# All loops of a three-layer kernel written out, and its clearing transfers issued by SyncE

## The reference, cut to what matters

```python
x = x + xattn(layernorm(x), ctx_512, Wq, w_kc_q, w_kc_kv, W_qr, W_kr, Wo)   # 16 heads, 257 context rows per batch item
x = x + attn(layernorm(x), wq, wk, wv, wo (codes and scales), biases)       # self attention, 32 tokens per batch item
x = x + ffn(layernorm(x), router_weight, gate_up_proj, down_proj)           # 64 experts, top 8, capacity 128

# ffn, cut:
probs = softmax(x @ router_weight.T)
topw, topi = top_k(probs, 8); topw = topw / sum(topw)
pos = place of each (token, expert) pair in its expert's list, in token order
xe = zeros((64, 128, 256)).at[expert, pos].set(x, mode='drop')
ye = (silu(xe @ gate) * (xe @ up)) @ down
y[token] = sum over the 8 pairs of topw * ye[expert, pos]
```

## Time and profile before

| | |
|---|---|
| time, median of 3 runs | 846.65 us (844.25 to 850.82) |
| span of the profiled execution | 876.3 us |
| instructions | 17897 |
| PE, DVE, ACT, POOL busy | 76%, 48%, 35%, 33% |
| bytes moved | 92.66 MB, mean 106 GB/s |
| fold and weights, pass 0 | 0 to 151 us |
| pass 1 | 157.9 to 218.6 us |
| passes 2 to 6 (the loop) | 218.7 to 537.4 us |
| pass 7 | 537.4 to 592.1 us |
| experts and output | about 666 to 876.3 us |

### The profile page before, as it was taken

How to read it: one execution, slowest core, us unless ns; L and a number is a source line. 1 busy time by engine, 2 the same in 40 slices (tenths; PEclk the granted TensorE clock), 3 DMA queues, 4 the chain that set the end, 5 groups by cost and what they waited for, 6 DMA issues and landing times.

```text
span 876.3 us, 17897 instructions
## 1 busy us (share of the span) xinstructions
PE 664.1 (76%) x6210; PEld 536.8 (61%) x6210; DVE 420.8 (48%) x1090; ACT 305.1 (35%) x811; POOL 291.6 (33%) x279
## 2 busy tenths in 40 slices
PE   7856777889999997997997997998714765556550
PEld 5745557777867875875875875867513654445440
DVE  1414663454765774774774764756441222222232
ACT  1122553235453362362362363350302333333210
POOL 4003584212114224124124122021224455555562
PEclk8855657799999998998998998999966999999985
DMA  8946994791002002002001001000004989998956
GB/s 244 253 84 154 251 221 120 247 344 27 1 2 79 0 8 70 0 15 63 0 15 63 0 22 38 3 30 30 24 26 120 227 190 200 198 196 198 203 95 168
DMA packets 100680, 92.66 MB, mean 106 GB/s; under 512 B 32366, under 2 KB 94576, under 8 KB 100640
## 3 DMA queue, kind: packets, MB, share of 16 engines
q1 hardware_dynamic: 70992, 60.87, 26.8%
q0 software_dynamic: 12288, 17.95, 10.0%
q10 hardware_dynamic: 17360, 13.30, 5.1%
HBM read 60.22 MB, written 32.83 MB: 106 GB/s over the span
## 4 chain that ended last, share of the span: by engine, by line
PE 42%; DMA 21%; DVE 14%; issue 10%; ACT 5%; another core or an unknown queue 3%; ACTq 2%; SPq 1%; POOL 1%; DVEq 0%; POOLq 0%; PEldq 0%
DMA expert_sums<-Wh,etok 18%; PE bank L1135 5%; PE bank L1137 5%; PE bank L1136 5%; PE bank L1169 4%; PE bank L1201 4%; PE bank L1190 3%; PE bank L1154 3%; PE bank L1238 3%; PE bank L1183 2%; PE bank L1112 1%; ACTq L564 1%; PE bank L1124 1%; PE bank L1182 1%
## 5 line engine op out<-in xcount | busy, mean ns | idle before, releaser
L530 POOL DMA_INDIRECT expert_sums<-Wh,etok x64 | 98.8, 1544 | 96.9 <-DVE Wh L1037 83.0
L1338 PE MATMUL bank<-ring,Wh 96*128 96x256 f32 x128 | 45.0, 434 | 66.1 <-DVE Wh L1025 64.5
L606 ACT ACTIVATE pr<-bank,nmax 128x257 f32<-128x257 f32 x128 | 61.2, 478 | 95.9 <-DVE nmax L830 94.7
L1135 PE MATMUL bank<-space,Wh 128*128 128x128 f16 x512 | 89.4, 221 | 4.9 <-DVE X L928 3.2
L473 POOL DMA_INDIRECT expert_rows<-h,slot x64 | 62.7, 980 | 87.2 <-DVE slot L921 66.6
L1137 PE MATMUL bank<-space,Wl 128*128 128x128 f16 x512 | 89.3, 220 | 0.0
L1136 PE MATMUL bank<-space,Wh 128*128 128x128 f16 x512 | 89.3, 220 | 0.0
L1201 PE MATMUL bank<-Cr,pT 128*128 128x64 f32 x512 | 78.9, 281 | 6.2 <-DVE On L840 5.3
L1201 PEld LDWEIGHTS bank<-Cr,pT 128*128 128x128 f32 x512 | 75.0, 211 | 8.2 <-DVE On L840 5.2
L456 POOL TENSOR_TENSOR Cr<-C,Ct 128x192 f32<-128x192 f32 x64 | 38.4, 625 | 115.9 <-PE bank L1201 114.6
L830 DVE TENSOR_REDUCE nmax<-bank 128x1 f32<-128x257 f32 x128 | 53.4, 419 | 48.6 <-PE bank L1183 43.8
(11 more groups left out here) (173 smaller groups left out, 1518.6 us busy)
## 6 DMA issues: line engine op xcount, KB each, us to landing
ring<-L_ffn_gate_up_proj_dram SPq DMA_DIRECT2D x64, 192.0 KB
expert_rows<-h ACTq DMA_DIRECT2D x8, 1284.0 KB, 13.8
Wh<-expert_rows SPq DMA_DIRECT2D x64, 160.5 KB
ring<-L_ffn_down_proj_dram SPq DMA_DIRECT2D x64, 96.0 KB
C<-ctx_dram SPq DMA_DIRECT2D x24, 128.0 KB, 4.0
expert_sums<-h ACTq DMA_DIRECT2D x2, 1152.0 KB, 14.0
space<-L_xattn_Wo_dram SPq DMA_DIRECT2D x8, 256.0 KB, 5.0
space<-L_xattn_Wq_dram SPq DMA_DIRECT2D x4, 512.0 KB, 8.3
```

The lines of the kernel that those rows point to most:

```text
L530: e.indirect_dma_start(Y[n % NY][:, :], bass.IndirectOffsetOnAxis(ap=etok[:, n % 4:n % 4 + 1], axis=0), ye[:, n % 4], None, bounds_check=Y ...
L606: e.activation(pr[:, s, :], bank[r % 2][:, 0:NL], ACT.Exp, bias=nmax[:, s:s + 1], accum_out=rsum[:, s:s + 1]).then_inc(expd, 1)
L1135: e.matmul(dst, ah, bh, start=first and n == 0, stop=False)
L1338: e.matmul(bank[4 + n % 2][:, 0:D], hh[:, n % 2], dn[:, n], start=True, stop=True).then_inc(e_dn, 1)
```

## The change

Every `e.Fori` loop on every engine becomes a Python `for`, so that its body is written out once for each iteration, and all waits and addresses are constants. `blank` is taken out of ACT's pass 1 and moved to SP, behind the wait for `w_done` and ahead of the loads of the first experts and of the contexts of tiles 2 to 7. SP first waits for `iotas`, the zeroed row.

```diff
@@ SP @@
+            def blank(n):
+                if n < E // 8:
+                    e.dma_start(XE.rearrange("(e c) d -> c e d", c=CAP)[:, 8 * n:8 * n + 8],
+                                h3[:, :].unsqueeze(1).to_broadcast([P, 8, ROW])).then_inc(zero_out, 16)
+                else:
+                    e.dma_start(Y[n - E // 8].rearrange("(a p) d -> p a d", p=P),
+                                h3[:, 0:D].unsqueeze(1).to_broadcast([P, YROWS // P, D])).then_inc(zero_out, 16)
+
+            e.wait_ge(iotas, 2)
+            for n in range(E // 8 + NY):
+                blank(n)
             for n in range(NB):
                 load_expert(n, n)
-            with e.Fori(2, T) as i:
+            for i in range(2, T):
                 e.wait_ge(roped, i * (2 * BT))
                 load_context(i)
@@ ACT, pass 1 @@
-                        if isinstance(i, int) and i == 1:
-                            if r == 0:
-                                e.wait_ge(iotas, 2)
-                            if r < E // 8 + NY:
-                                blank(r)
@@ PE, ACT, DVE (POOL alike), the pipeline @@
-            with e.Fori(1, T - 2) as j:
+            for j in range(1, T - 2):
                 tile(j + 1, j, j - 1)
@@ POOL (SP, PE, ACT, DVE alike), the experts @@
-            with e.Fori(1, E // NB) as j:
+            for j in range(1, E // NB):
                 add_out(j, False)
```

More of the change, by code:

```diff
@@ L565, in _ @@
                     e.dma_start(obias[:, :], bo.unsqueeze(0).to_broadcast([P, D])).then_inc(bias_in, 16)
[L567 to L574, removed]
             def x_use(name, i):
@@ L705, in _ @@
             expert_copy(0, 0)
-            with e.Fori(0, E // NB - 1) as j:
+            for j in range(E // NB - 1):
                 experts(j, False)
@@ L1351, in _ @@
             experts(0, True, False)
-            with e.Fori(1, E // NB - 1) as j:
+            for j in range(1, E // NB - 1):
                 experts(j, False, False)
```

## The result

The changed kernel takes 869.36 us, the median of 4 runs (867.0 to 877.9), beside 846.74 us for the kernel before in the same comparison. The ratio is 1.027, with an interval from 1.021 to 1.033: slower.

A forecast was written before the change was run, and what follows sets the result against it. The prediction took PE to bound the tile pipeline and the adding DMAs the experts. A late context (23.9 us) less ACT's gain (1.4), loops worth nothing, adds 22.5 to 846.65: 869 us, range 838 to 878.

The forecast's parts named there:

- The deciding term: SP's queue: tile 2's context lands near 193 us behind 12.88 MB of clearing, so DVE waits 23.9 us more in pass 1.
- ACT's gain: ACT, pass 1: without the clearing issues its stalls go, worth 1.4 us by comparing PE's time in passes 1 and 2.
- The bound of 13 us: ACT, pass 1: upper bound of the saving, at most four issue stalls of up to 4.33 us.
- The two cancel: PE, pass 1: q products done during the wait (2.7 us) against a lower clock (2 to 5 us), together zero, 3 either way.
- The waits at the ends of passes 3 to 6: PE in later passes: 26.2 us over pass 2's pace, taken as the profiled execution's, so straight code gains nothing.
- The loops' waits are real: Rival, ends of passes 3 to 6: straight code gains 26.2 us against 22.5, giving 843 us; chance 0.18.
- The context is not late: Rival, SP's queue: the wait stays hidden, leaving only ACT's 1.4 to 13 us, 834 to 845 us; chance 0.09.
- The delay is longer: Rival, pass 1: SP stalls per issue and 1.2 GHz clock persists, or code fetches: 879 us and more; chance 0.09.

The follow-up runs named there:

- context first: Changed kernel, but SP loads the context of tile 2 ahead of the clearing: 848.15 us, ratio 0.995 to the kernel before; repeated, 849.33 us, 0.994.
- move alone: Kernel before with its loops kept, only the clearing transfers moved from ACT to SP: 874.41 us, ratio 1.029; repeated, 875.67 us, 1.032.
- first chip: Chip of the first follow-up comparison; the unchanged kernel before takes 849.99 us there (29 runs).
- loops alone: Kernel before with all loops written out, ACT still issuing the clearing: median 858.26 us, ratio 0.996; repeated, 856.07 us, 1.014.
- third chip: Chip on which the changed kernel, its two halves and the version with the early context ran again; the kernel before takes 852.13 us (13 runs).
- the first comparison: The whole change against the kernel before: 869.36 us beside 846.74 us, ratio 1.027.
- second chip: Chip of the runs with POOL's order changed, three or six clearing transfers ahead, or context between clearing and experts; kernel before 874.75 us.

## Why the prediction was right, and where its steps were off

**The deciding term held.** The context of tile 2 queues behind 12.88 MB and is there at 188.5 us, where 193 was taken and 189 to 194.8 were the ends. It came just under the fast end. Part of that is SP's start at 139.5, not 141.8, so that the distance from SP's first issue is 49.1 for an expected 51 us (52.2 to 53.3 in the three other profiles of this order). DVE waits 22.23 us (26.7 to 28.3 in the others) for an expected 23.9. Four kernels show that this is the cause: moving the context alone removes the loss, changing POOL's order alone removes DVE's wait with the context still late, and of the clearing transfers three ahead leave 1.45 us of wait and six 12.18 us and 15.0 us more time.

**ACT's gain was too small: 1.4 us taken, 4.8 to 7.0 measured.** The step that failed is the comparison of the rest of pass 1 with the rest of pass 2 (45.1 and 43.7 us, "the same PE work to within 7 of 484 products"). Measured from the start of the scaling in the first `normalise` to the start of the last product, pass 2 of the kernel before takes 39.35 us, with PE busy for 36.53 (468 products), and pass 1 takes 37.11, with PE busy for 35.42 (461 products), once the stalls are gone. The seven further products, most of them the router's, and 1.1 us more of idle time make pass 2 some 2.2 us too long to be pass 1's floor. In the profile that the prediction had read, this stretch of pass 1 takes 40.81 us, 3.7 above those 37.11. The bound of 13 us was not reached. The timed medians of the same two pairs differ by 10.1 and 6.7 us, but their ratios by 0.1% and 1.9%: the profiles show the gain on both chips, the ratios on one.

**"The two cancel" was not separable, and the sum still came out.** Behind the hole the changed kernel needs 36.91 us from the scaling to the last product (413 products, 48 having been done during the wait), and the kernel with the context first 37.11 (461 products). So the work done ahead and the lower clock do cancel, to 0.2 us. The 0.82 that the prediction read as the sign of a pause is from a stretch in which PE is idle for 3.3 of 38 us only the earlier trace rows; for a hole of 20 us the fall to one half is shown here, by the 0.50 from 178 to 190 us. By the profiles the change of pass 1 is then +23.5 - 7.6 = 15.9 us (move alone against before, first chip) or +25.6 - 5.2 = 20.4 (changed kernel against loops alone, third chip): start of the scaling later, stretch behind it shorter. Timed, these pairs are 24.4 us (874.41 less 849.99) and 18.6 us (874.62 less 856.07) apart. The forecast of 22.5 lies between. In the first pair the profile of before was taken in a run of 859.22 us, 9.2 above the median; the two profiled runs themselves are 14.9 us apart, which the 15.9 fit. That the forecast met the 22.6 of the first comparison to a tenth is luck: the gain was taken 3 to 6 us too small. Two of the forecast's own signs show the same: DVE's product was to start near 198 us and started at 193.01, and pass 1 was to end near 241 and ended at 234.2 us.

**The waits at the ends of passes 3 to 6: right in its use, wrong as put.** I took them for something that the profiled execution has and the timed runs hardly have, and not for the loops' doing. That loops don't make them is shown: looped passes without them on two chips, straight ones with them on another. But they are no accident of single executions. On the second chip every profile has them and the median of the 19 runs of before is some 25 us longer, the size of the 26.2 us. The first profile therefore seems to come from such a chip and the three times from another, which is an inference; on the changed kernel's own chip the waits are absent. On the second chip the kernels without a late context were 1.5% faster than before. Whether that is the straight code (its waits there are 1.7 us and not 4.5), or ACT's 5 to 7 us, or both, isn't told apart: the loops alone did not run there.

**The rivals.** *The loops' waits are real* would have given 843 us; there are looped passes without them and straight ones with them, and the loops written out alone show no gain on two chips. Whether straight code is faster on the second chip is open. *The context is not late* falls with POOL's row at 188.52. *The delay is longer*: the clock was one half from the hole on, but from 198 to 205 us it is 0.97 again here (0.52 with the move alone, and 1.00 from 205 on), so the cold stretch stayed short.

**The best version** is the context first, with SP clearing: 0.995 and 0.994 of before, with intervals that end at 0.999 and 1.000, and medians 1.8 and 2.8 us below. That is a gain of some 0.5%, less than the 5 to 7 us of ACT's stalls would give alone. The version with loops in it, which the straight code has not beaten anywhere, was not run.

## What to carry to other kernels

Before a bulk transfer is moved to a less busy engine, list what stands behind it in that engine's queue, and find for each the first instruction that waits for it and what stands behind that instruction on its own engine: here a transfer that had 12 us of slack met a delay of 32. Put the small transfer that someone waits for ahead of the bulk; here that cost nothing that shows. And price a stall by a stretch with the same instructions without it, not by the same number of them.

## What the hardware showed that I had not expected

- A queue with bulk transfers in it holds the issuing sequencer: ten issues took 30.4 us of SP (139.45 to 169.85), 3.6 to 5.0 us each from the fourth on. The first small load behind them still took 4.12 us, and those from the third on 0.43 to 0.54.
- One and the same kernel differs by chip: 850, 852 and 875 us for the kernel before. The four other kernels that were profiled on the chip with the 875 us have waits ahead of PE's last product in passes in which POOL issues scatters, and a wait of 9.1 us later. That the 25 us lie there is an inference.
- On one chip the runs of one kernel spread by up to 24 us (840.37 to 864.05 for the loops alone). The cause is open. Some of the difference between profiles lies ahead of anything that was changed: SP reaches the place of the change between 138.57 us (context first, third chip) and 145.26 us.
- PE's clock after the hole: PE starts again at 194.63, the granted clock from 190 to 198 us is 0.50, and from 198 to 205 us it is 0.97 in the changed kernel, with PE busy throughout. With the move alone PE starts again at 199.86, and the granted clock is 0.52 from 198 to 205 us and 1.00 from 205 to 210.
